# Routing with its bias on VectorE, an earlier first batch and scatters moved behind the slots; a sweep with shorter index steps

## The reference, cut to what is computed

```python
xn = layernorm(x)
def arma_conv(x, src, dst, init_w, w, root_w, b):       # K = 2 stacks, T = 3 rounds
    norm = dinv[src] * dinv[dst]                        # deg ** -0.5
    root = einsum('nf,kfg->nkg', x, root_w)
    for t in range(3):
        h = einsum(x, init_w) if t == 0 else einsum('nkf,kfg->nkg', out, w)
        out = relu(segment_sum(h[src] * norm, dst) + root + b)
    return out.mean(axis=1)
h = relu(arma_conv(xn, ..., w1)); latent = relu(arma_conv(h, ..., w2))
rec = relu(latent @ fc1_w + fc1_b) @ fc2_w + fc2_b
k, v = layernorm(heads(xn @ wk.T)), layernorm(heads(xn @ wv.T))   # 4 heads of 64
mix = (heads(xn @ wq.T) @ (k^T v / S)) @ wo.T + bo
x = x + rec + mix
f = layernorm(x)
p = softmax(relu(f @ router_w1 + router_b1) @ router_w2 + router_b2)
top_w, top_i = top_k(p, 2); weights = softmax(top_w)
x = x + sum over the two of weights * expert(f)          # 256 -> 256 -> 256 -> 256, relu between
```

## Time and profile before

| | |
|---|---|
| median of the runs | 3560.35 us (3555.49 to 3562.27) |
| profiled execution | 3588.53 us, span 3586.6 us, mean granted clock 0.97 |
| PE busy | 3356.3 us, 94% of the span |
| PEld | 1949.6 us |
| DVE | 1291.1 us, 36% |
| ACT | 736.0 us, 21% |
| POOL | 275.9 us, 8% |

### The profile page before, as it was taken

The page is one execution under the profiler, slowest core; times in us unless marked ns, Lnnn a source line. Parts: engine busy times, 40 slices in busy tenths (PEclk is TensorE's granted clock), DMA queues, the critical chain, the costliest instruction groups (busy, mean ns, idle before and its releaser), DMA issues. The chain is left out here.

```text
span 3586.6 us, 49904 instructions
## 1 busy us (share of the span) xinstructions
PE 3356.3 (94%) x18034; PEld 1949.6 (54%) x18035; DVE 1291.1 (36%) x4555; ACT 736.0 (21%) x1502; POOL 275.9 (8%) x277
## 2 busy tenths in 40 slices
PE   6998999999989999995999999999999997939999
PEld 3574556555545555553555555555555554726776
DVE  7747777777711111111111111212121003534444
ACT  3445555555500000000000000000000000513333
POOL 3000000000000000000000000000000002264333
PEclk9997999999999999998999999999999999969999
DMA  7212322333289999999644447988888995237775
GB/s 196 67 47 79 142 120 114 152 152 136 100 335 308 303 307 309 299 309 291 189 145 151 148 153 245 331 283 282 287 283 290 303 302 188 80 130 250 244 246 191
DMA packets 262110, 761.06 MB, mean 212 GB/s; under 512 B 25971, under 2 KB 178476, under 8 KB 259926
## 3 DMA queue, kind: packets, MB, share of 16 engines
q1 hardware_dynamic: 171512, 616.10, 51.2%
q10 hardware_dynamic: 78814, 115.44, 12.5%
q0 software_dynamic: 11648, 27.76, 2.1%
HBM read 532.00 MB, written 239.86 MB: 215 GB/s over the span
## 5 line engine op out<-in xcount | busy, mean ns | idle before, releaser
L1506 PE MATMUL acc<-stage,split 128*128 128x448 f16 x5488 | 1044.6, 353 | 4.8 <-PEq L1457 4.8
L1506 PEld LDWEIGHTS acc<-stage,split 128*128 128x128 f16 x5488 | 537.3, 98 | 502.7 <-PEq L1457 5.1
L1506 PE MATMUL acc<-stage,other 128*128 128x448 f16 x4116 | 784.4, 353 | 0.0
L1211 PE MATMUL first_sum<-stage,other 128*128 128x448 f16 x2744 | 647.5, 353 | 0.2 <-ACT stage L1029 0.2
L1506 PEld LDWEIGHTS acc<-stage,other 128*128 128x128 f16 x4116 | 403.1, 98 | 378.1 <-issue 7.7
L1567 DVE TENSOR_TENSOR tmp<-acc,dinv_b 128x448 f32<-128x448 f32 x98 | 61.0, 623 | 1287.4 <-PE acc L1506 1287.4
L1029 ACT ACTIVATE stage<-group_ps 128x392 f16<-128x392 f32 x784 | 386.3, 497 | 308.4 <-PE group_ps L1200 304.8
L1075 DVE TENSOR_SCALAR place<-iota_col,rel 128x196 f16<-128x196 f16 x1568 | 349.9, 266 | 0.0
L1211 PEld LDWEIGHTS first_sum<-stage,other 128*128 128x128 f16 x2744 | 253.0, 98 | 137.7 <-issue 1.1
L1072 DVE TENSOR_TENSOR lanes<-iota_two,lane_two 128x256 f16<-128x256 f16 x784 | 226.4, 289 | 87.5 <-PE group_ps L1200 72.2
L1433 ACT ACTIVATE split<-r,b_two 128x448 f32 x14 | 8.9, 633 | 1156.8 <-issue 680.8
(11 more groups left out here) (342 smaller groups left out, 2547.3 us busy)
## 6 DMA issues: line engine op xcount, KB each, us to landing
stage<-adj_d SPq DMA_DIRECT2D x490, 784.0 KB, 4.3
adj_d<-stage SPq DMA_DIRECT2D x14, 5488.0 KB, 17.9
row_d<-blank ACTq DMA_DIRECT2D x20, 3340.5 KB, 62.9
other<-pack_d SPq DMA_DIRECT2D x42, 898.0 KB, 5.0
part_d<-blank ACTq DMA_DIRECT2D x10, 3340.5 KB, 61.9
slot_rows<-row_d SPq DMA_DIRECT2D x42, 393.0 KB, 5.5
rin<-root_d SPq DMA_DIRECT2D x28, 448.0 KB, 7.6
slot_base<-row_d SPq DMA_DIRECT2D x21, 393.0 KB, 6.0
```

What stands on the lines that cost most here:

```text
L1211: m = mm(acc[b][k][:, 0:WIN], other[:, h, half, k * P:(k + 1) * P], stage[b][:, h, :], start=(h == 0 and half == 0), stop=(h == TILES - 1 ...
L1506: m = nc.tensor.matmul(acc[b][k][:, :], src[:, h, part, k * P:(k + 1) * P], ring[:, i, r, :], start=(h == 0 and part == 0), stop=(h == TIL ...
```

## The change

In the sweep: `LAG` 39 instead of 38 (88 steps), sums `SUB`+4 steps behind, two buffers of squares, x in four parts (the second, 7 tiles, on ACT's queue; the last behind SP's new wait for all near gathers), `tables` at DVE's start, and columns that fold the hits twice in half precision before the reduction. `RUN_AT`, `TURN_AT` and `DEG_AT` become 9, 25 and 33; the seven later columns run in seven steps in a row instead of every second one; `flags` moves ahead of `split_codes`, four steps earlier. In the first pass, `finished` is dealt out over groups 4 to 9, and the set-up `scales` moves from group 0 to 4. In the last pass ACT loads x and transposed x of batch 0 into an unread part of `other` (`ahead`). In routing DVE adds the bias of all batches, POOL sends 56 scatters (set 0 both ways, sets 1 and 2 first only), set 2's ranking, weights and seats go ahead of batch 6's routing, and SP no longer waits for the first list. In the experts SP loads two weight packs first, then waits for the first list; POOL sends 7 first-list scatters and 8 second-list ones at once, and three second-list ones ahead of each of nine slots. The diff, cut:

```diff
-            LAG = 38
+            LAG = 39
+            SUM_LAG = SUB + 4
             EVEN = FULL // 16 * 16
             QUAD = 4
             STEPS = TILES + LAG
             CUMS = G + 1
             XB = RUNS // P
-            PARTS = ((0, SUB), (SUB, 3 * SUB), (3 * SUB, TILES))
-            RUN_AT, TURN_AT, DEG_AT = 7, 24, 32
+            PARTS = ((0, SUB), (SUB, 2 * SUB), (2 * SUB, 4 * SUB), (4 * SUB, TILES))
+            RUN_AT, TURN_AT, DEG_AT = 9, 25, 33
...
+                    for q in range(PAIRS):
+                        sp.wait_ge(e_near[q], 32)
                     sp.wait_ge(e_pad, 4)
...
                     def column(k):
                         e.then(nc.vector.tensor_scalar(hit[:, :, :], near_rel[:, :, :], k - 0.5, None, ALU.is_lt))
-                        e.then(nc.vector.tensor_reduce(cum[:, :, k], hit[:, :, :], X, ALU.add))
+                        for n in (REACH // 2, REACH // 4):
+                            e.then(nc.vector.tensor_tensor(hit[:, :, 0:n], hit[:, :, 0:n], hit[:, :, n:2 * n], ALU.add))
+                        e.then(nc.vector.tensor_reduce(cum[:, :, k], hit[:, :, 0:REACH // 4], X, ALU.add))
...
-                        if j == 2:
+                        if j == 1:
                             dve.wait_ge(n_in[1], 16)
                             measured(*PARTS[1])
+                            scattered(1)
                         if j == 3:
-                            scattered(1)
-                        if j == 4:
                             scales(1)
                         if j == 5:
-                            tables()
-                        if j == 6:
                             ordered()
-                        if j == 12:
-                            dve.wait_ge(n_in[2], 32)
-                            measured(PARTS[2][0], 5 * SUB)
-                        if j == 14:
-                            measured(5 * SUB, TILES)
+                        if j == 8:
+                            dve.wait_ge(n_in[2], 16)
+                            measured(2 * SUB, 3 * SUB)
+                        if j == 9:
+                            measured(3 * SUB, 4 * SUB)
                             scattered(2)
-                        if j == 16:
+                        if j == 11:
                             scales(2)
+                        if j == 17:
+                            dve.wait_ge(n_in[3], 32)
+                            measured(4 * SUB, 5 * SUB)
+                        if j == 19:
+                            measured(5 * SUB, 6 * SUB)
+                        if j == 21:
+                            measured(6 * SUB, TILES)
+                            scattered(3)
+                        if j == 24:
+                            scales(3)
                         if j == RUN_AT:
                             near_shifted()
                         if j == RUN_AT + 1:
@@ -685,17 +702,17 @@
                         if j == RUN_AT + 2:
                             column(4)
                             starts()
-                        turn, odd = divmod(j - RUN_AT - 3, 2)
-                        if odd == 0 and 0 <= turn < 7:
-                            column((1, 2, 3, 5, 6, 7, 8)[turn])
+                        if RUN_AT + 3 <= j < RUN_AT + 10:
+                            column((1, 2, 3, 5, 6, 7, 8)[j - RUN_AT - 3])
                         if j == RUN_AT + 10:
+                            flags()
+                        if j == RUN_AT + 11:
                             split_codes()
                         if j == RUN_AT + 12:
                             lanes_known()
+                        if j == RUN_AT + 13:
+                            rows_known()
                         if j == RUN_AT + 14:
-                            rows_known()
-                        if j == RUN_AT + 16:
-                            flags()
                             keys_known()
...
-                        if j >= 1:
-                            act.wait_ge(f_red, j)
-                        nc.scalar.activation(sq[:, :, :], kv_ps[:, :, :], ACT.Square).then_inc(f_ke, 1)
+                        if j >= 2:
+                            act.wait_ge(f_red, j - 1)
+                        nc.scalar.activation(sq[:, j % 2, :, :], kv_ps[:, :, :], ACT.Square).then_inc(f_ke, 1)
...
-                            if w >= 2 and at == 4:
-                                finished((w - 2) // 2, w % 2)
+                            if w >= 2 and 4 <= at < 10:
+                                finished((w - 2) // 2, w % 2, (at - 4) // 3, (at - 4) % 3)
...
+                act.wait_ge(p_free, PIECES + LAST_PASS * WINS * PIECES)
+                act.dma_start(x_ahead, a["x"][0:SUB * P, :].rearrange("(j p) f -> p j f", p=P)).then_inc(g_in, 16)
+                act.dma_start(xT_ahead, xnT_d.rearrange("p (k n) -> p k n", k=2)[:, :, 0:ROW]).then_inc(g_in, 16)
...
-                    for i in range(1, BATCHES):
-                        own = rows[:, i * SUB:(i + 1) * SUB, 0:D]
-                        pool.wait_ge(l_x[i], 32 if i == BATCHES - 1 else 16)
-                        nc.gpsimd.tensor_tensor(own, own, bias[:, 0, :].unsqueeze(1).broadcast_to([P, SUB, D]), ALU.add).then_inc(l_xb, 1)
...
                     scattered(0, 0, l_first)
                     scattered(0, 1, l_second)
                     scattered(1, 0, l_first)
-                    scattered(1, 1, l_second)
                     scattered(2, 0, l_first)
-                    scattered(3, 0, l_first)
...
+                    ranked(2)
                     routed(BATCHES - 1)
                     logits(BATCHES - 1)
-                    ranked(2)
...
+                    def biased(i):
+                        own = rows[:, i * SUB:(i + 1) * SUB, 0:D]
+                        if i >= 1:
+                            dve.wait_ge(l_x[i], 32 if i == BATCHES - 1 else 16)
+                        tt(own, own if i >= 1 else ahead[0], bias[:, 0, :].unsqueeze(1).broadcast_to([P, SUB, D]), ALU.add).then_inc(l_xb, 1)
...
+                        if i + 1 < BATCHES:
+                            biased(i + 1)
...
+                    sets[2].weights()
+                    sets[2].seated()
                     logits_in(BATCHES - 1)
                     sets[3].peaks()
-                    sets[2].weights()
-                    sets[2].seated()
...
+                for s in range(2):
+                    pack_in(s, s)
+                sp.wait_ge(l_first, 16 * TILES)
                 for s in range(BUF):
                     rows_in(s, s)
-                for s in range(2):
-                    pack_in(s, s)
...
+                for j in late_first:
+                    token(j, 0, l_first)
+                AT_ONCE, EACH = 8, 3
+                for j in late_second[0:AT_ONCE]:
+                    token(j, 1, l_second)
...
                 for s in range(STEPS):
+                    for j in late_second[AT_ONCE + s * EACH:AT_ONCE + (s + 1) * EACH]:
+                        token(j, 1, l_second)
```

146 lines of the change are left out of this document (83 added, 63 removed).

## The result

The changed kernel takes 3520.5 us as the median of four runs (3520.1 to 3521.0), against 3560.3 for the kernel before: 39.8 us less, a ratio of 0.989 (95% interval 0.9873 to 0.9907). The forecast was 3504 with a range of 3488 to 3526, so the time lies in the range, and the gain is 0.7 of what the sum said.

A forecast was written before the change was run, and what follows sets the result against it. PE was taken as mostly busy, with recoverable waits in the sweep, first pass and routing: -8.6 - 15.6 - 31.8 = -56.0 us, from the median 3560.35 to 3504, range 3488 to 3526.

The forecast's parts named there:

- Sweep: Pass over the 49 tiles: less DVE index work and recovered idle time gain 8.6 us, ends 3 and 16.
- The fold: DVE's index columns: two half-precision additions before a shorter reduction, 2.4 against 2.7 us a column, 2.8 us less over nine.
- SP's new wait: SP waits for near gathers before later loads and root stores: priced at nothing, a few us if the cover is gone.
- First pass: First pass over windows: dealing out `finished` and moving `scales` gain 15.6 us, ends 8 and 16.
- the stall: First pass over windows: PE's 12 waits for DVE's `place`, one per window, all go, worth 15.1 us.
- Cost 0: Last pass: ACT's 1.8 MB loads for batch 0 beside the matrix stream cost nothing, upper end 6 us.
- Routing, front half: Start of routing: bias on VectorE and batch 0 loaded early bring batch 1 20.2 us earlier, net 17.9.
- Routing, tail: End of routing to first expert matmul: 3192.1 against 3223.86, 31.8 us gained including 17.9 from earlier; ends 38 and 24.
- Experts: Expert slots: POOL's three extra tokens in nine steps take 7.5 us, inside PE's pace of 8.4; cost 0.
- (2): First pass over windows: projections wait in place of `place`, the pass gives 8 us, total 3512; chance 0.08.
- The slower rival: Experts: POOL's scatters stretch beside DVE to over 3.0 us each and set the step; 3571 at 3.1; chance 0.03.
- The rule against the change: Routing: VectorE's fast-mode copies block GpSimd's scatter descriptors, speaking against bias beside scatters; no row showed it, no size given.

The follow-up runs named there:

- the second pair: The kernel before and the changed kernel, both unedited, executed and profiled again on another, slower chip of the same kind: 3617.3 and 3573.8 us.
- rows_early: Changed kernel with SP storing a pair's finished rows ahead of its wait for the window's hidden rows: 3556.4 us, against 3573.8 for the changed kernel executed again.
- pool_bias: Changed kernel with GpSimd adding the bias of batches 1 to 6 again in routing: 3596.7 us, 22.9 above the changed kernel executed again.

## Why the prediction was right or wrong

- **Sweep**: right, and in its size with some luck. -8.7 against -8.6 (-8.9 in the second pair), a column of 2.41 against 2.4. But step 26 started 9.9 earlier, not 9.0, and the longer lag took 1.2 back, not 0.4; the two misses cancel. The fold is about 1.6 of it, where the prediction had 2.8. SP's new wait cost nothing visible: no wait of ScalarE for a store of root terms stands in the trace after.
- **First pass**: wrong, -3.3 (and -2.4) against -15.6. The failed step is "So the stall goes, all 12: 15.1 us. Late next is the row projection", and the pass also lies below the lower end of 8. The stall did go where no rows are stored; what came late next was not the projection but SP's store of finished rows, which waits for the last step of `finished` and stands behind two loads. I had counted the queue that the moved steps feed (TensorE's) and not the one that waits on them (SP's). rows_early shows both the cause and the size: with the store early the pass falls by a further 16.2.
- **Passes**: "Cost 0" holds for the last pass, in which TensorE is as full as before (busy 260.2 of its last 263 us, against 260.76). Unforeseen is the root projection's wait. It gave 6 to 7 us between the usual executions (13.7 against 7.6 and 6.6), without a known cause, and 26 us more in the first pair of profiles.
- **Routing, front half**: right. Batch 1's turn 20.3 us earlier against 20.2; the first scatter 17.3 earlier against 17.9.
- **Routing, tail**: near. One_ps after 193.2 us against 191.3 in the sum. The last scatters of the stage start 3.4 us later than reckoned (149.1 after the stage's start against 145.7), the drain took 4.6 us behind the last scatter instead of 6.4.
- **Experts**: the step fits, with 0.8 to 1.0 us to spare as forecast, and costs nothing on the first chip. On a chip with the standstills it costs 8.3.
- **The end**: missed. The last drain, 6.5 us longer, had no row in the prediction; of POOL's queue I had followed the drain at the end of routing only.
- **The sum**: -8.7 + 1.4 - 3.3 - 6.9 - 29.9 - 0.7 + 6.5 = -41.6, against 39.8 measured, where -6.9 is the passes' difference without the 26.1 us of the long wait. Of the 56.0 in the prediction the first pass gave 12.3 too little, routing 1.9; the end (6.5) and the block boundary ahead of the first pass (1.4, in both pairs, its cause open) had no term. The root projection, which had none either, made up 6.9 of it. That is luck: without it the time would be 3527, just outside the range.
- **Rivals**: (2) is nearest to what happened, a first pass that gives less, but it had 8 us left of it where 3.3 were, and it named another wait. The slower rival needed 3.0 us a scatter in the experts: there the tokens stayed 1.27 to 1.45 us apart on all chips. Its mechanism was looked for at GpSimd; on the other chips it was the remaining engines that stood still while GpSimd sent.
- **The rule against the change** (the Trainium skill, SBUF — State Buffer, SBUF: two separate sides: VectorE's copies in its fast modes keep GpSimd from writing descriptors): something like it is seen, for the bias addition too. The scatter that starts beside an addition takes 2.7 to 2.8 us instead of 0.97, in all eleven executions with the additions on VectorE, and no scatter takes so long in the two of the kernel before or in pool_bias. It cost nothing on the first chip: it struck two scatters, and GpSimd then waited 2.81 and 3.23 us for its next lists.

## What to carry to other kernels

When steps are dealt out, list everybody that waits for the last of them, the engine that only issues transfers first, and look what stands behind that wait in its list: here the dealing-out gave 1.7 us until a store stood earlier, and 17.0 then. Before a sum is made on one profile, compare its execution with the median and find the wait that makes the difference, so that it isn't counted as the kernel's. A queue that is emptied at the end of the program is part of the time: moving sends behind other work saved 23.6 us in one stage and paid 14.8 in two others, on a chip with the standstills.

## What the runs showed of the hardware

- While GpSimd sends indirect transfers, TensorE, VectorE and ScalarE stood still for 3 to 17 us at a time on three chips, without a releaser in the trace, and never on the first one; routing took 267 and 223 us in the same kernel.
- An indirect scatter of GpSimd took 0.97 us, and 2.7 to 2.8 when it started beside a VectorE addition of 2.02 us on two single-precision operands of 128x1792.
- GpSimd's queue drained in 4.6 us at the end of the program, and in 11.1 when tokens had been sent between the slots' scatters; with as many sent ahead of them it was 4.6.
- Behind some waits of TensorE of 2.0 to 3.0 us the granted clock stood at 0.50 for 3.2 us or a little more (0.97 over 49 us), behind others of up to 3.04 us it stayed at 1.00, and behind waits of 1.26 us always.
- One wait behind 30 fills on ScalarE's DMA queue took 13.7 and 39.8 us in two executions of the kernel before and 6.5 to 9.5 in nine of the changed kind.
